# A three-layer graph network on one core: rings of three residues in the node stages, first node weights loaded during the norm, last one-hot rows issued by ACT

## The reference

```
def layer(edge_index, x, edge_attr, norm, We, be, Wn, bn):
    parts = [x[src], x[dst]] (+ [edge_attr] after the first layer)
    e     = relu(concat(parts) @ We + be)               # 50000 x 128
    msg   = e * norm[:, None]
    agg   = segment_sum(msg, dst, num_segments=3125)
    x_new = relu(concat([x, agg]) @ Wn + bn)            # 3125 x 128
    return x_new, e

x = layernorm(x + gru_network(x))        # first network, five steps
x = layernorm(x + three_layers(x))       # _L1_gnn_ref, weights We0..We2, Wn0..Wn2
```

## Time and profile before

| what | us |
|---|---|
| median of three runs | 2377.35 |
| the profiled execution, its own time | 2376.61 |
| its span, first to last instruction | 2374.4 |
| first norm | 940.5 to 965.1 |
| first node stage | 965.3 to 996.6 |
| first edge pass, with its overflow tile | 997.7 to 1409 |

### The profile page before, as it was taken

One profiled execution on the slowest core, in us unless ns is written; L12 is line 12 of the kernel. 1 busy time (PEld: TensorE's weight loads), 2 busy tenths in 40 slices (PEclk: granted clock), 3 DMA queues, 4 the chain that ended last, 5 costly groups with the idle time before them and its releaser, 6 DMA issues. The chain is left out here.

```text
span 2374.4 us, 50364 instructions
## 1 busy us (share of the span) xinstructions
PE 2020.9 (85%) x14516; PEld 1445.6 (61%) x14516; DVE 1455.5 (61%) x4548; ACT 662.9 (28%) x1344; POOL 1063.3 (45%) x1086
## 2 busy tenths in 40 slices
PE   7687776999999997398888866999999769999983
PEld 4221113454544543287777755999999659888881
DVE  6888873132322323687878846767777467777774
ACT  0145663121211211332333324323233231111111
POOL 0444430000000000377777736777777267777770
PEclk7767767999999998699999978999999889999996
DMA  3022445000000001544444425777777345555541
GB/s 91 14 49 67 87 83 47 0 0 0 0 0 0 0 0 44 209 132 142 143 145 142 144 77 136 210 209 207 209 205 210 93 127 146 146 140 144 142 121 30
DMA packets 188937, 242.83 MB, mean 102 GB/s; under 512 B 53217, under 2 KB 115068, under 8 KB 188076
## 3 DMA queue, kind: packets, MB, share of 16 engines
q1 hardware_dynamic: 155420, 173.31, 25.4%
q0 software_dynamic: 32864, 60.32, 11.1%
q10 hardware_dynamic: 432, 6.29, 0.6%
HBM read 150.92 MB, written 69.26 MB: 93 GB/s over the span
## 5 line engine op out<-in xcount | busy, mean ns | idle before, releaser
L1504 POOL DMA_INDIRECT rows<-p_dram,src_i x912 | 893.0, 979 | 305.1 <-issue 257.4
L1737 DVE TENSOR_TENSOR agg_t<-psum,agg_t 128x128 f32 x1368 | 390.2, 285 | 153.2 <-PE psum L1621 122.9
L1603 PE MATMUL psum<-w_c,before 128*128 128x128 f32 x1824 | 403.6, 303 | 0.0
L1672 ACT ACTIVATE rows<-rows 128x512 f32<-128x512 f32 x228 | 143.7, 630 | 754.6 <-DVE rows L1730 750.5
L884 PE MATMUL psum<-adj,parts 128*128 (+2 forms) x1750 | 339.7, 351 | 5.6 <-ACT agg L963 4.4
L1721 DVE TENSOR_SCALAR hot_w<-col_f,dst_loc,weight 128x128 f32<-128x128 f32 x912 | 319.1, 354 | 0.3
L664 PE MATMUL psum<-src_hot,dst_hot 128*128 128x391 f16 x586 | 228.0, 432 | 81.3 <-ACT psum L686 27.5
L1603 PEld LDWEIGHTS psum<-w_c,before 128*128 128x128 f32 x1824 | 279.7, 194 | 0.0
L1264 POOL MEMSET agg_t<- 128x3200 f32 x1 | 2.8, 2766 | 606.5 <-POOLq L1020 606.5
L1621 PE MATMUL psum<-hot_w,rows 128*128 128x128 f32 x1824 | 247.3, 279 | 29.8 <-ACT rows L1672 25.8
L884 PEld LDWEIGHTS psum<-adj,parts 128*128 128x128 f16 x1750 | 153.0, 98 | 191.1 <-issue 23.4
(11 more groups left out here) (249 smaller groups left out, 2504.3 us busy)
## 6 DMA issues: line engine op xcount, KB each, us to landing
e_dram<-after SPq DMA_DIRECT2D x228, 256.0 KB
before<-e_dram SPq DMA_DIRECT2D x228, 256.0 KB
adj<-stage SPq DMA_DIRECT2D x196, 97.8 KB, 3.5
pair_rows<-sorted_rows SPq DMA_DIRECT2D x114, 128.0 KB, 4.3
rows<-p_dram,src_i POOLq DMA_INDIRECT x912
hot_all<-dst_rows SPq DMA_DIRECT2D x1, 3584.0 KB, 12.5
hot_all<-dst_rows ACTq DMA_DIRECT2D x1, 3072.0 KB, 17.3
hot_all<-dst_rows ACTq DMA_DIRECT2D x1, 2048.0 KB, 10.5
```

The costliest lines, as they stand in the source:

```text
L1504: nc.gpsimd.indirect_dma_start(out=rows[:, b % ROWS, m * D:(m + 1) * D], out_offset=None, in_=p_dram, in_offset=bass.IndirectOffsetOnAxis( ...
L1603: mm = nc.tensor.matmul(o, before[:, q % BEFORE, m * P:(m + 1) * P], w_c[:], start=False, stop=True)
L1672: nc.scalar.activation(e_of(q), source, ACT.Relu).then_inc(e_on, 1)
L1737: nc.vector.tensor_tensor(a, psum[:, A_BANKS[q % len(A_BANKS)], m * P:(m + 1) * P], a, ALU.add).then_inc(agg_on, 1)
```

## The change

Three edits. (1) In every node stage both residue rings get three buffers, and DVE waits for the reader three back. (2) `w_ab`, `b_rep_e` and a semaphore `first_in` are made in `build`, and the loads of We0 and be0 are issued by SP in the norm, behind the loads of x, and not at the start of the first node stage. PE and DVE wait for `first_in` at the place where they waited before. (3) The fourth piece of `hot_all` is issued by ACT as its first DMA in the first edge pass, behind its table load, and no longer by SP at the end of the first node stage.

```diff
@@ build
+        keep["w_ab"] = sb("w_ab", [P, 2 * D], F32)
+        keep["b_rep_e"] = sb("b_rep_e", [P, D], F32)
+        keep["first_in"] = ctx.enter_context(nc.semaphore("first_in"))
-        add_and_norm(nc, "_0", x1, x, None, psum, keep, hT, dst_rows)
+        add_and_norm(nc, "_0", x1, x, None, psum, keep, hT, dst_rows, weight_loads(keep, None, (We0, be0)))
@@ add_and_norm, block.sync, behind the loads of x
+            for to, dram in first_loads:
+                sp.dma_start(to, dram).then_inc(keep["first_in"], 16)
@@ node_stage
-        residue = sb("residue_q", [P, 2, 2, D], F32)
-        residue_p = sb("residue_p", [P, 2, 2, D], F32)
+        RESIDUES = 3
+        residue = sb("residue_q", [P, RESIDUES, 2, D], F32)
+        residue_p = sb("residue_p", [P, RESIDUES, 2, D], F32)
@@ node_stage, block.sync
-            for to, dram in loads:
-                sp.dma_start(to, dram).then_inc(w_in, 16)
...
-                if tables is not None:
-                    load_hot(sp, t["hot_all"], t["hot_in"], dst_rows, len(HOT_CHUNKS) - 2)
                 sp.wait_ge(stored, 16 * len(starts))
@@ node_stage, block.tensor and block.vector
-            if loads:
-                pe.wait_ge(w_in, 16 * len(loads))
+            if tables is not None:
+                pe.wait_ge(keep["first_in"], 48)
@@ node_stage, block.vector
-                if i >= 2:
-                    dve.wait_ge(p_low, i - 1)
-                nc.vector.tensor_tensor(residue_p[:, i % 2, 0:k, :], p_sb[:, a:a + k, :],
+                if i >= RESIDUES:
+                    dve.wait_ge(p_low, i - RESIDUES + 1)
+                nc.vector.tensor_tensor(residue_p[:, i % RESIDUES, 0:k, :], p_sb[:, a:a + k, :],
...
-                if i >= 2:
-                    dve.wait_ge(low, i - 1)
-                nc.vector.tensor_tensor(residue[:, i % 2, 0:k, :], bank(i, 1), q_parts[:, a:a + k, 0, :],
+                if i >= RESIDUES:
+                    dve.wait_ge(low, i - RESIDUES + 1)
+                nc.vector.tensor_tensor(residue[:, i % RESIDUES, 0:k, :], bank(i, 1), q_parts[:, a:a + k, 0, :],
@@ edge_pass, block.scalar
             nc.scalar.preload_act_table(ACT.Relu)
+            if is_first:
+                load_hot(nc.scalar, hot_all, t["hot_in"], dst_rows, len(HOT_CHUNKS) - 2)
```

More of the change, by code:

```diff
@@ L1158, in edge_layers @@
         t["hot_all"], t["hot_in"] = keep["hot_all"], keep["hot_in"]
-        for name, shape in (("w_n", [P, 2, D]), ("b_n", [P, 1]), ("w_ab", [P, 2 * D]), ("b_rep_e", [P, D])):
+        t["w_ab"], t["b_rep_e"] = keep["w_ab"], keep["b_rep_e"]
+        for name, shape in (("w_n", [P, 2, D]), ("b_n", [P, 1])):
             t[name] = sb(name, shape, F32)
@@ L1165, in edge_layers @@
                      for i in range(2)]
-        first_loads = weight_loads(t, None, weights[0][0:2])
-        node_stage(nc, "_first", False, True, psum, hT, t, p_dram, first_loads, tables, dst_rows, keep)
+        node_stage(nc, "_first", False, True, psum, hT, t, p_dram, tables, keep)
         for l, (We, be, Wn, bn) in enumerate(weights):
@@ L1173, in edge_layers @@
                       over_dram[l - 1] if l else None, over_dram[l] if more else None,
-                      weight_loads(t, (Wn, bn), weights[l + 1][0:2] if more else None))
+                      weight_loads(t, (Wn, bn), weights[l + 1][0:2] if more else None), dst_rows)
             node_stage(nc, f"_{l}", True, more, psum, hT, t, p_dram)
@@ L1191, in weight_loads, with node_stage @@
     return loads
-def node_stage(nc, tag, update, products, psum, hT, t, p_dram, loads=(), tables=None,
-               dst_rows=None, keep=None):
+def node_stage(nc, tag, update, products, psum, hT, t, p_dram, tables=None, keep=None):
     with ExitStack() as ctx:
@@ L1323, in second_part @@
                 act.wait_ge(resid, i + 1)
-                nc.scalar.activation(q_parts[:, a:a + k, 1, :], residue[:, i % 2, 0:k, :],
+                nc.scalar.activation(q_parts[:, a:a + k, 1, :], residue[:, i % RESIDUES, 0:k, :],
                                      ACT.Copy).then_inc(mid, 1)
@@ L1332, in second_source_part @@
                 act.wait_ge(p_resid, i + 1)
-                nc.scalar.activation(p_parts[:, a:a + k, 1, :], residue_p[:, i % 2, 0:k, :],
+                nc.scalar.activation(p_parts[:, a:a + k, 1, :], residue_p[:, i % RESIDUES, 0:k, :],
                                      ACT.Copy).then_inc(p_mid, 1)
@@ L1373, in _ @@
                         ALU.min).then_inc(turned_on, 1)
-            if loads:
-                dve.wait_ge(w_in, 16 * len(loads))
+            if tables is not None:
+                dve.wait_ge(keep["first_in"], 48)
             for i, pair in enumerate(pairs):
@@ L1392, in edge_pass @@
 def edge_pass(nc, tag, nth, Wc, psum, keep, t, is_first, p_dram, e_before, e_after, over_before,
-              over_after, next_loads):
+              over_after, next_loads, dst_rows):
     with ExitStack() as ctx:
```

7 lines of the change are left out of this document (3 added, 4 removed).

## The result

The changed kernel takes 2372.08 us (median of 17 runs, 2369.14 to 2374.53), the kernel before 2377.86 us in the 17 runs beside them. The ratio is 0.9975 with a 95% interval of 0.9968 to 0.9981, that is 5.8 us less; 6.5 were forecast. The total agrees better than its parts do: by the trace the weights brought more than their 3.2 us, and the moved load of `hot_all` brought next to none of its 3.4. The two misses have opposite signs, and that the total lies near the forecast is in part luck.

The account below looks back on a forecast made before the run. A chain of blocks, each bound by its longest engine: POOL in the first edge pass, DVE in the node stage's steady part. 0 + 3.2 + 3.4 less 0.1 gave 6.5 us: 2377.35 - 6.5 = 2370.9 us, range 2369.8 to 2378.2.

Parts of the forecast that it names:

- Part 1: Rings of three in the node stages: nothing gained, 0 us, bounds 0.1 us either way in each of three stages.
- Part 2: First node stage: weights loaded in the norm end PE's wait for `b_rep_e`, 3.2 us gained, least 0, most 3.4.
- the first products cost what they cost now: First node stage: granted clock 0.50 on both sides of the move, so the whole stage comes 3.2 us earlier.
- Part 3: Start of first edge pass: moving the last `hot_all` load removes POOL's wait, 3.4 us gained if `pair_rows` gets ahead.
- what an engine has begun of the large load, it carries to the end: DMA queues in the first edge pass: read from 62 of 63 packets being q1's, none a gather's, from 998.4 to 1003 us.
- depends on who reaches the DMA engines first: Start of first edge pass: `pair_rows` issued ahead of the large load, so `pair_hot` after 3.55 to 5 us, under 6.3.
- the limit of 6.3: First edge pass: `pair_hot` must start within 6.3 us for POOL's wait to go entirely, the whole 3.4 us.
- ACT's own part: First edge pass: ACT's issue is free, 0.05 us behind `pair_rows`, or 1.28 us if ACT waits for its table load.
- B: Rival: `pair_rows` partly waits for the large load, `pair_hot` 8 to 12 us in, POOL waits 2 to 5: 2372.9 to 2376; 0.08.
- "slower": Whole kernel: chance 0.03 of a slower time, for something that none of the cases has.
- The secondary claim: First edge pass: slot 3's `pair_hot` 13.2 us after the large load, PE's slot 3 at 1008.6, holding by 0.8 us.
- The marks: Profile signs: no `b_rep_e` wait, edge pass near 994.5, `pair_hot` under 6.3 us, no L1599 wait, gather at about 1031.

Follow-up runs that it names:

- 4: The changed kernel with all four pieces of `hot_all` issued by ACT in the norm, none in the first edge pass: 2371.33 us, ratio 0.9965.
- 9: The changed kernel itself once more, on a chip like the first: 2371.41 us, ratio 0.9971 to the kernel before.
- 12: The changed kernel with the large load issued by SP behind the first two `pair_rows` and the next weights, on a chip like the first: 2369.31 us, ratio 0.9961.
- 10: The changed kernel with all four pieces of `hot_all` issued by ACT in the norm, on a chip like the first: 2368.91 us, ratio 0.9958.
- 11: The changed kernel with the large load issued by ACT behind the relu of slot 2, on a chip like the first: 2369.84 us, ratio 0.9963.
- 2: The kernel before with only the first node weights loaded in the norm: 2374.34 us, ratio 0.9981.
- 3: The kernel before with only the last piece of `hot_all` moved to ACT's first DMA in the first edge pass: 2378.45 us, ratio 0.9993.
- experiment 1: The kernel before with only the rings of three residues in all node stages: 2379.25 us, ratio 1.0002.

## Why the prediction was right, and where it was wrong

**Part 1, right.** 0 was said, and the rings alone give 1.0002 (0.9993 to 1.001).

**Part 2, right in its mechanism, too small in its sum.** The wait of 3.2 us went as said (3.39 at the first product). The stage behind it was taken as fixed, "the first products cost what they cost now". They don't. Time from the first product to the start of the edge pass, against when the granted clock rose from 0.50 to 1.0, in nine profiles of the first kind of chip:

| kernel | clock rose, from the first product | product to edge pass, us |
|---|---|---|
| 4, 9, 12 | already up | 25.89 each |
| changed, 10, 11 | 2 to 2.2 us later | 26.89, 26.98, 26.97 |
| before, 2 | 4.4 to 4.6 us later | 28.05, 27.95 |
| 3 | 5.8 us later | 28.17 |

So a stage of nearly the same instructions (with or without the issue of the large load at its end, rings of two or three) takes 25.9 to 28.2 us, and the changed kernel's profile had 1.16 us of that beside the term of the sum. The rise falls differently from run to run of the same kernel (9 and the changed kernel are the same code). The profiles without the wait stand at 25.89 to 27.95, those with it at 28.05, 28.17 and 28.38 (experiment 1, clock up 5.2 us later). That the wait itself puts the rise off is therefore likely, but three profiles don't show it, and experiment 2 rose as late without the wait. The 4.5 us of the weights alone, with their interval of 2.6 to 6.7, hold the 3.2 as well.

**Part 3, wrong.** 3.4 us were forecast if `pair_hot` starts within 6.3 us of the pass; it started at 9.28, 8.36 and 10.05. The step that failed is the reading of the earlier trace rows: "what an engine has begun of the large load, it carries to the end", and with it that the outcome "depends on who reaches the DMA engines first". The rows showed only q1 packets while POOL's gathers stood issued, and I read that as an engine that finishes one queue's load before it serves another. But the gathers may have had nothing in their queue yet: after, where the queues do take turns, their first packet too comes 5.0 us behind their first issue (1000.38 against 995.38; before it was 4.6, 1003.05 against 998.42). So the row said nothing on how queues share, and "the trace agrees" was too much. Where both queues hold packets, as after, they go one for one. In what I called forecast (`pair_rows` ahead), `pair_rows` was ahead, and it gained by that only the two of its eight packets that had gone before the first large one.

The Trainium skill (DMA: Bandwidth & Descriptors, section "Queues, rings and completion order") says that an engine goes round its queues and changes at the bounds of a packet. I took from it only that nobody passes a packet. The other half, that each queue gets its turn after one packet, is what the trace after shows: 44 packets against 43. The page also puts some 9 to 17 descriptors into a packet. That doesn't show here for pieces of 28 KB: an engine carried 5.8 of them in all before `pair_hot` started, and q1 was served all the while.

From rows of before the price could have been bounded: 62 packets of q1 took 99.9% of 16 engines for 4.6 us, 1.19 us for one of 28 KB, and 8 turns of one such packet are up to 9.5 us on top of the undisturbed 3.55. Measured were 5.8 us on top, and anything over 2.8 is past the limit of 6.3.

**ACT's own part, right.** 0.05 us behind `pair_rows` was said for the case that a table load is treated like an activation: it was 0.03. The section "What ACT_TABLE_LOAD costs" (the Trainium skill, ScalarE: Activation LUTs) has a drain of 1380 ns; the DMA behind the load isn't held by it, since its issue started 0.02 us after the load's start.

**The rivals.** What happened in part 3 is B, `pair_hot` 8 to 12 us into the pass and POOL waiting 2 to 5 us, to which I gave 0.08. Its mechanism (a few descriptors wait for a part of the load) was nearer than that of the forecast. Its time, 2372.9 to 2376, is at the least 0.8 above the 2372.08 measured; the 1.16 us that part 2 brought beyond its term cover that. The chances of the cases add up to 1 with the forecast, so the 0.03 for "slower" for something that none of the cases has is counted beyond them. The secondary claim, slot 3 at 1008.6, failed with it: the second `pair_hot` started 15.0 us into the pass, where I had 13.2, and with no harm, since POOL hadn't the lead that would have needed it.

**The marks.** No wait for `b_rep_e`: right. The edge pass at 994.5: 994.67, with the norm 1.5 us later than before. `pair_hot` under 6.3 us: wrong. No wait of POOL for L1599: wrong. The gather that was at 1037.69 at about 1031: it came at 1034.31, less the norm's 1.51 us that is 1032.8, so 4.9 us were gained there of the 6.6.

**The sum.** Forecast 0 + 3.2 + 3.4 - 0.1 = 6.5. By the trace 0 + 4.55 + about 0.4 = 5.0 at POOL's release (71.40 - 66.48 us from the norm = 4.92), and 5.8 by the medians, where the interval of the ratio is 4.5 to 7.6 us. The time came out near the forecast for a reason that is half wrong: of the 3.4 us of part 3 some 3 are missing, and 1.2 us of an early rise of the clock, which no term had, make up for part of them. Where the other 0.8 us between the trace and the medians lies isn't shown; it is within their interval.

## What to carry to other kernels

A transfer that shares the DMA engines with a large one of another queue paid here for about one large packet per packet of its own that hadn't gone when the large load began (5 to 7 of 8 on each engine): count its packets per engine, multiply by the time of one large packet, and take that as the most it can lose, whoever is issued first. Keep urgent small loads clear of such a load by issuing the large one when the small ones have landed, or cut its packets down. And where a stage of a few tens of us is to change by 1 or 2 us, read the granted clock through its first products, since a single profile holds that much of chance.

## What the runs showed of the hardware

- Two queues with work shared the DMA engines packet for packet, unlike as the packets were: 44 packets of 1 KB against 43 of 28 KB in 3 us. In experiment 10, in the first node stage (970 to 974 us), the tables and the load of `hot_all` do not divide so evenly:

```profile
q10 hardware_dynamic: 63, 1.81, 104.6%
q1 hardware_dynamic: 32, 0.04, 2.7%
```

Half as many packets of q1 as of q10 are there; whether q1 had something to send all the time, the row doesn't show.
- A DMA issued by ACT behind a table load started 0.02 to 0.03 us after that load had begun, in three profiles (changed kernel, experiments 3 and 9).
- From the start of the ninth gather to that of the last of 304 it took 376.1 to 381.1 us in profiles of the first kind of chip, with the same code in that stretch, with a median gather of 944 to 947 ns; this is the spread against which a gain of 3 us in this pass must be told.
